# A linear-attention stage regrouped: 256 rows of each of two sequences, side by side in the partition halves

## The chip, the cores and the metric

The kernel runs on one NeuronCore of a Trainium2 chip. The core has five engines with instruction queues of their own: TensorE (PE in the profile; PEld is its loading of stationary operands), VectorE (DVE), ScalarE (ACT), GpSimd (POOL) and SyncE (SP, which here only issues DMAs). They meet through semaphores. The metric is the time of one execution in microseconds on the device; a run is repeated and the median compared. A profiled execution gives the trace; its span runs from the first to the last instruction.

## The reference

`x` is (4, 1024, 128) in float32. Four residual layers follow one another; the change is in the first two, and only in the first one's arithmetic order.

```python
# layer 1: linear attention, B=4, T=1024, D=128, H=64; xn = layernorm(x)
q, k, v = phi(xn @ W_q), phi(xn @ W_k), xn @ W_v        # phi(a) = elu(a) + 1
S_t = S_{t-1} + k_t v_t^T ;  z_t = z_{t-1} + k_t         # per sequence
o_t = (S_t q_t) / max(z_t . q_t, 1e-6)
x = x + o @ W_o
# layer 2: mixture of experts, E=8, top-1; xn = layernorm(x)
logits = xn @ router_W + router_b ; e = argmax(logits) ; gate = softmax(logits)[e]
x = x + gate * (relu(xn @ W1[e] + b1[e]) @ W2[e] + b2[e])
# layer 3: a gated token mix with a scan over time; layer 4: the experts again
```

## The kernel before

The 4096 rows are 32 tiles of 128. A **group** is four tiles, 512 rows in a row of one sequence, so a sequence has two groups and there are eight (`NG`). All work of a layer is written out by hand as slots, one list per engine: in slot `k` of `attn_slot` each engine does steps of several groups, `project_qk(k)`, `project_out(k-2)`, `score_and_turn(k-1)` and so on for PE, `add_attention(k-2)`, `mask_scores(k-1)`, `phi(k)`, `scan_z(k)` for DVE. Within an engine this order is fixed; between engines `wait_ge` on a counting semaphore holds a step until its input is there and the buffer it writes is free.

For a group the steps are these. ACT normalises the rows (`norm`), PE turns them (`transpose_x`), ACT copies them out (`evac_xT`). `project_qk` makes q in partitions 0 to 63 and k in 64 to 127 of `bank[1]`, 512 columns; `project_v` makes v in partitions 0 to 63 and the eight "old" router scores (those of the rows before attention's output is added) in 64 to 71 of `bank[2]`. ACT and DVE make phi of q and k (`phi_parts`, `phi`, tile `qk`). `score_and_turn` multiplies v by q for each tile (`L1621`), turns k (`turn_k`, `L1614`) and v with the old scores (`L1640`) so that rows lie in partitions (`kv`). DVE masks the scores (`am`, `L1088`). `updates_and_intra` forms the state updates (`L1660`, into partitions 0 to 63 of `bank[5]`) and the products inside a tile (`L1649`, into 64 to 127). `add_state` (`L1096`, `L1099`) adds the state that the sequence's first group left, and `read_inter` (`L1676`) multiplies it by q. `scan_z` (`L1114`) is the running sum of k on 64 partitions, `z_dot_q` on POOL (`L499`) multiplies it by q. `project_out` (`L1693`) takes both, stacked in `op`, through `wox`, which holds ones for the sum of z.q, `w_o`, and `w_o` times the router. `add_attention` (from `dmax`, `L950`) divides and adds to the rows.

Behind that, for the experts: `measure_choose_and_add_state` takes the row's moments, the logits and the one-hot choice `oh` (`L902`), `count` on PE (`L1586`, `L1590`) counts choices, `placed` gives each row its place, and POOL sends rows to a sorted buffer in HBM, tile by tile (`send_tiles`). Column `IDC` of the rows holds each row's number in `x`; the experts' results are scattered by it. The first expert tiles start when the first four groups have been sent.

SP issues all loads in one list: x, the output weights, the mixing weights (`rwo`, `rwr`, `rwv`, `vec`), then `b2b`, `w1all`, `w2s`. PE waits for the mixing weights in `setup_transposes`, which stands inside `score_and_turn(0)`. `warm_up` and `keep_clock` are matmuls that only keep TensorE busy.

Every float32 matmul appears in the trace as two passes, a transpose as one.

## Time and profile before

| | us |
|---|---|
| median of 3 runs (295.75 to 297.28) | 297.17 |
| the profiled execution | 295.25 |
| its span, first to last instruction | 293.5 |
| mean granted TensorE clock, share of 2.4 GHz | 0.994 |
| busy in the span: PE / DVE / POOL / ACT | 276.7 / 231.8 / 225.1 / 187.5 |

The attention stage is the first 77 us of the span. "Busy" counts an engine's own instructions; issuing DMAs, waiting and branching are not in it. A duration of a matmul in the trace includes its way through the array, so passes that follow one another overlap in the records.

### The profile page before, as it was taken

How to read it: one execution, taken by the hardware profiler on the slowest of the kernel's cores; microseconds unless marked ns; L12 is line 12 of the kernel's file. 1: busy time of each engine (PE TensorE's matmuls, PEld its weight loads, DVE VectorE, ACT ScalarE, POOL GpSimd, SP SyncE). 2: the span in 40 equal slices, each digit the busy share in tenths (PEclk: the TensorE clock that was granted, in tenths of full speed). 3: DMA queues.
4: the chain of work that ended last, by engine and by line, in shares of the span. 5: the costliest groups of instructions: out<-in, count | busy, mean ns of one | idle time of the engine just before them, and what ended most of it. 6: DMA issues, size and time to landing. Idle time of an engine off the chain costs nothing.

```text
span 293.5 us, 7743 instructions
## 1 busy us (share of the span) xinstructions
PE 276.7 (94%) x2177; PEld 243.1 (83%) x2177; DVE 231.8 (79%) x1019; ACT 187.5 (64%) x565; POOL 225.1 (77%) x302
## 2 busy tenths in 40 slices
PE   7999999988789999999999999999899999999994
PEld 7666666666489999999996479988698999999994
DVE  4889799999688698777874278999965997777773
ACT  2776666540289788888881166755378887666661
POOL 3967378889768888888555584788878888889775
PEclk9999999999799999999999999999999999999999
DMA  6998910000341563542100920011315235432210
GB/s 177 236 352 239 109 33 31 28 28 30 75 96 47 122 127 87 115 100 67 40 24 5 245 48 0 28 40 37 82 59 122 65 103 123 110 89 72 65 40 6
DMA packets 32522, 25.70 MB, mean 88 GB/s; under 512 B 6001, under 2 KB 28786, under 8 KB 32481
## 3 DMA queue, kind: packets, MB, share of 16 engines
q1 hardware_dynamic: 27328, 16.54, 25.5%
q0 software_dynamic: 4576, 8.57, 8.7%
...
q14 instruction: 23, 0.18, 0.2%
q10 hardware_dynamic: 576, 0.10, 0.2%
...
## 4 chain that ended last, share of the span: by engine, by line
PE 66%; DVE 17%; POOL 5%; issue 4%; DMA 3%; ACT 3%; SPq 0%; POOLq 0%; ACTq 0%
PE pair L1835 21%; PE pair L1821 13%; PE bank L1821 6%; PE bank L1706 4%; POOL sorted L517 3%; PE bank L1811 3%; PE pair L1748 3%; PE pair L1701 2%; PE pair L1601 2%; PE pair L1755 2%; DVE zT L1114 2%; DMA xs<-sorted 2%; PE pair L1693 2%; DMA sorted<-rows,place 2%; PE bank L1576 2%
## 5 line engine op out<-in xcount | busy, mean ns | idle before, releaser
L1835 PE MATMUL pair<-w2s,hT 128*128 x624 | 82.9, 276 | 0.3
L517 POOL DMA_INDIRECT sorted<-rows,place x64 | 66.7, 1043 | 18.3 <-issue 14.6
L1835 PEld LDWEIGHTS pair<-w2s,hT 128*128 128x128 f32 x624 | 75.7, 192 | 0.9 <-issue 0.6
L1821 PE MATMUL pair<-xsT,w1s 128*128 128x128 f32 x406 | 57.0, 276 | 0.9 <-ACT xsT L770 0.9
L1821 PEld LDWEIGHTS pair<-xsT,w1s 128*128 128x128 f32 x406 | 50.9, 192 | 2.0 <-issue 1.0
L693 ACT COPY w1s<-w1all 128x516 f32 x78 | 49.7, 638 | 0.6 <-issue 0.6
L540 POOL DMA_INDIRECT x_mid<-ys,xs x39 | 38.4, 985 | 14.4 <-DVE ys L1378 9.8
L540 POOL DMA_INDIRECT out<-ys,xs x39 | 38.4, 985 | 9.1 <-issue 7.2
L770 ACT COPY xsT<-bank 128x128 f32<-128x128 f32 x78 | 20.8, 266 | 36.8 <-PE bank L1811 35.7
L1368 DVE SCALAR_TENSOR_TENSOR ys<-pair,xs 128x128 f32<-128x128 f32 x78 | 26.9, 345 | 18.3 <-PE pair L1835 18.1
L775 ACT ACTIVATE hT<-pair,w1s 128x128 f32<-128x128 f32 x117 | 34.7, 374 | 1.1 <-PE pair L1821 1.1
L775 ACT ACTIVATE hT<-bank,w1s 128x128 f32<-128x128 f32 x109 | 32.6, 377 | 0.0
L1338 DVE TENSOR_SCALAR xsn<-xs 128x128 f32<-128x128 f32 x78 | 27.9, 360 | 5.6 <-DMA xs<-sorted 5.6
L1349 DVE SCALAR_TENSOR_TENSOR xs<-b2b,xs 128x128 f32<-128x128 f32 x78 | 27.3, 349 | 6.1 <-issue 3.3
L1821 PE MATMUL bank<-xsT,w1s 128*128 128x128 f32 x218 | 30.8, 276 | 0.4 <-ACT xsT L770 0.4
L491 POOL TENSOR_TENSOR rows<-veps,neg_half 128x4 f32<-128x4 f32 x16 | 21.3, 1334 | 9.0 <-ACT veps L649 8.8
L1358 DVE TENSOR_SCALAR hT<-pair,w1s 128x128 f32<-128x128 f32 x86 | 27.5, 345 | 0.6
L1821 PEld LDWEIGHTS bank<-xsT,w1s 128*128 128x128 f32 x218 | 27.4, 192 | 0.7 <-ACT xsT L770 0.7
L1811 PE MATMUL bank<-ident,xsn 128*128 128x128 f32 x78 | 21.4, 274 | 0.6 <-DVE xsn L1338 0.6
...
L637 ACT COPY xnT<-bank 128x512 f32<-128x512 f32 x16 | 9.5, 592 | 14.8 <-PE bank L1576 14.7
L1748 PE MATMUL pair<-wx,xnT 128*128 128x256 f32 x64 | 15.7, 389 | 0.7 <-ACT xnT L637 0.7
...
## 6 DMA issues: line engine op xcount, KB each, us to landing
...
sorted<-rows,place POOLq DMA_INDIRECT x64, 2.4
x_mid<-ys,xs POOLq DMA_INDIRECT x39, 2.6
```

The source lines that it names most:

```text
L517: pool.indirect_dma_start(sorted_rows[l], bass.IndirectOffsetOnAxis(ap=place[:, t:t + 1], axis=0), rows[:, t, :], None).then_inc(s_sent[l] ...
L540: pool.indirect_dma_start(x_new[l], bass.IndirectOffsetOnAxis(ap=xs[b][:, IDC:IDC + 1].bitcast(I32), axis=0), ys[b][:, 0:(XM, D)[l]], None ...
L693: nc.scalar.copy(w1s[i % NW][:], w1all[:, bass.ds(e, 1), :].rearrange("p o f -> p (o f)")).then_inc(s_w1, 1)
L775: last = nc.scalar.activation(hT[i % NB][:, c], bank[2 + i % 2][:, c * P:(c + 1) * P], ACT.Relu, bias=w1s[i % NW][:, DF + c:DF + c + 1])
L1338: nc.vector.tensor_scalar(xsn[i % NB][:], xs[b][:, 0:D], xs[b][:, MEAN:MEAN + 1], xs[b][:, RSTD:RSTD + 1], ALU.subtract, ALU.mult).then_in ...
L1349: nc.vector.scalar_tensor_tensor(out=xs[b][:, 0:D], in0=b2b[:, bass.ds(e, 1), :].rearrange("p o d -> p (o d)"), scalar=xs[b][:, GATE:GATE ...
L1358: last = nc.vector.tensor_scalar(hT[i % NB][:, c], bank[4 + i % 2][:, f:f + P], w1s[i % NW][:, DF + c:DF + c + 1], 0.0, ALU.add, ALU.max)
L1368: nc.vector.scalar_tensor_tensor(out=ys[b][:, 0:D], in0=bank[6 + i % 2][:, 0:P], scalar=xs[b][:, GATE:GATE + 1], in1=xs[b][:, 0:D], op0=AL ...
L1748: nc.tensor.matmul(mix_to(g, j), xnT[p][:, j * P:(j + 1) * P], wx[:].rearrange("p w d -> p (w d)"), start=(j % 2 == 0), stop=False, skip_g ...
L1811: nc.tensor.transpose(bank[0][:, 0:P], xsn[i % NB][:], ident[:]).then_inc(s_xsT, 1)
L1821: mm = nc.tensor.matmul(bank[2 + 2 * half + i % 2][:, c * P:(c + 1) * P], w1s[i % NW][:, f:f + P], xsT[i % NB][:], start=True, stop=True)
L1835: mm = nc.tensor.matmul(bank[6 + i % 2][:, 0:P], hT[i % NB][:, c], w2s[:, bass.ds(e, 1), c, :].rearrange("p o d -> p (o d)"), start=(c == ...
```

## The change

A group becomes 256 rows of each of two sequences (`HW = 256`; four chunks in a sequence, `CHUNKS`). Tiles 0 and 1 of a group belong to the first sequence, tiles 2 and 3 to the second. What stood in 64 partitions by 512 columns now stands in 128 by 256, the first sequence in partitions 0 to 63 and the second in 64 to 127. q and k lie side by side in columns. The products of the two sequences are separate matmuls on different halves of TensorE's rows or columns: `project_qk` four with 64 stationary columns, scores, updates, intra and inter products one per sequence. The running state and the sum z go through four groups instead of two. k is turned two tiles at a time, v likewise, and the old scores are made with the router as the stationary operand (`wr32`, padded to 32 columns), one matmul per tile into its own 32 partitions, and are turned with the third transpose. In `project_out` the output and the sum z.q are no longer stacked: each tile takes one matmul from `ob` and one with a single moving column from `zq`. The groups' loads of x are two DMAs each; `IDC` gets the new order of rows and, between the layers, the old one again.

```diff
-vT = [sb(f"vT{p}", [VC, GW]) for p in range(2)]
-kv = [sb(f"kv{p}", [P, GT, KC]) for p in range(2)]
-zT = [sb(f"zT{p}", [H, GW]) for p in range(2)]
-op = [sb(f"op{p}", [P, GW]) for p in range(2)]
+vT = [sb(f"vT{p}", [P, HW + P]) for p in range(2)]
+kt = [sb(f"kt{p}", [P, GT // 2, P]) for p in range(2)]
+vt = [sb(f"vt{p}", [P, 3, P]) for p in range(2)]
+zT = [sb(f"zT{p}", [P, HW]) for p in range(2)]
+zq = [sb(f"zq{p}", [P, HW]) for p in range(2)]
+ob = [sb(f"ob{p}", [P, HW]) for p in range(2)]
-state = [sb(f"state{p}", [H, GT, H]) for p in range(2)]
+state = [sb(f"state{p}", [P, GT // 2, H]) for p in range(2)]
...
 def _(sp):
     def load_x(l, g):
+        if l == 0:
+            pair, c = divmod(g, CHUNKS)
+            src = x_tok.rearrange("(r s c j p) d -> p r s c j d", s=2, c=CHUNKS, j=GT // 2, p=P)
+            for s in range(2):
+                t = g * GT + 2 * s
+                sp.dma_start(rows[:, t:t + 2, 0:D], src[:, pair, s, c]).then_inc(s_x_in[g], 16)
+            return
-        sp.dma_start(rows[:, tiles(g), 0:(D, XM)[l]], src[:, tiles(g), :]).then_inc(s_x_in[g], 16)
+        sp.dma_start(rows[:, tiles(g), 0:XM], src[:, tiles(g), :]).then_inc(s_x_in[g], 16)
     def load_xs(l, i):
...
-            sp.dma_start(wo_lo[:], w_o).then_inc(s_wo, 16)
+            sp.dma_start(wox[0:H, 0:D], w_o).then_inc(s_wo, 16)
...
-        nc.gpsimd.iota(column(IDC, slice(0, NT)).bitcast(I32), pattern=[[P, NT]], base=0,
+        nc.gpsimd.iota(column(IDC, slice(0, NT)).bitcast(I32),
+                       pattern=[[2 * T, B // 2], [HW, CHUNKS], [T, 2], [P, GT // 2]], base=0,
     def scales(S, b):
...
-        nc.gpsimd.tensor_tensor(op[p][0:H, :], zT[p][:], qk[p][0:H, :], ALU.mult).then_inc(AS["zq"], 1)
+        nc.gpsimd.tensor_tensor(zq[p][:], zT[p][:], qk[p][:, 0:HW], ALU.mult).then_inc(AS["zq"], 1)
     def old_logits(g):
-        nc.gpsimd.tensor_tensor(lold[:, tiles(g)], kv[g % 2][:, :, H:VC], per_tile(std1[:, tiles(g)], GT),
+        scores = vt[g % 2][:, 2].rearrange("p (j c) -> p j c", j=GT)[:, :, 0:E]
+        nc.gpsimd.tensor_tensor(lold[:, tiles(g)], scores, per_tile(std1[:, tiles(g)], GT),
     def rows_ready(l, S, g):
...
+    for s in range(len(STAGES[0])):
+        pool.wait_ge(s_sent[0][s], 16 * (rows_of_stage(0, s) + (s == 0)))
+    nc.gpsimd.iota(column(IDC, slice(0, NT)).bitcast(I32), pattern=[[P, NT]], base=0,
+                   channel_multiplier=1).then_inc(s_const, 1)
+    pool.wait_ge(s_const, 3)
...
-        nc.scalar.copy(vT[g % 2][:], bank[2][0:VC, :]).then_inc(AS["v"], 1)
+        nc.scalar.copy(vT[g % 2][:], bank[2][:, 0:HW + P]).then_inc(AS["v"], 1)
     def evac_kv(g):
-        nc.scalar.copy(kv[g % 2][:, :, VC:KC], bank[1][:, 0:GT * H].rearrange("p (j c) -> p j c", j=GT))
-        nc.scalar.copy(kv[g % 2][:, :, 0:VC], bank[3][:, 0:GT * VC].rearrange("p (j c) -> p j c", j=GT)
+        nc.scalar.copy(kt[g % 2][:], bank[1][:, 0:HW].rearrange("p (j c) -> p j c", c=P))
+        nc.scalar.copy(vt[g % 2][:], bank[3][:, 0:3 * P].rearrange("p (j c) -> p j c", c=P)
     def evac_o(g):
-        nc.scalar.copy(op[g % 2][H:P, :], bank[5][H:P, :]).then_inc(AS["oe"], 1)
+        nc.scalar.copy(ob[g % 2][:], bank[5][:, HW:GW]).then_inc(AS["oe"], 1)
     def turned_weights():
...
+    act.wait_ge(s_zeroed, 2)
+    act.wait_ge(s_wc_act, 1)
+    nc.scalar.copy(wr32[:, 0:E], wc[:, 3 * H:3 * H + E]).then_inc(s_wc_act, 1)
...
-        nc.vector.tensor_tensor(am[:], bank[4][:].rearrange("p (j t) -> p j t", j=GT),
-                                causal[:].unsqueeze(1).to_broadcast([P, GT, P]), ALU.mult).then_inc(AS["am"], 1)
+        for s in range(2):
+            last = nc.vector.tensor_tensor(am[:, 2 * s:2 * s + 2],
+                                           bank[4 + s][:, 0:HW].rearrange("p (j t) -> p j t", t=P),
+                                           causal[:].unsqueeze(1).to_broadcast([P, GT // 2, P]), ALU.mult)
+        last.then_inc(AS["am"], 1)
     def add_state(g):
-        n = GT if g % 2 == 0 else GT - 1
+        n = 2 if g % CHUNKS < CHUNKS - 1 else 1
-        upd = bank[5][0:H, 0:H * n].rearrange("v (j k) -> v j k", j=n)
-        if g % 2 == 0:
-            nc.vector.tensor_copy(state[0][:], upd).then_inc(AS["state"], 1)
+        upd = bank[4][:, HW:HW + H * n].rearrange("v (j k) -> v j k", j=n)
+        if g % CHUNKS == 0:
+            nc.vector.tensor_copy(state[g % 2][:, 0:n], upd).then_inc(AS["state"], 1)
-            nc.vector.tensor_tensor(state[1][:, 0:n], upd, state[0][:, GT - 1:GT].to_broadcast([H, n, H]),
+            nc.vector.tensor_tensor(state[g % 2][:, 0:n], upd, state[1 - g % 2][:, 1:2].to_broadcast([P, n, H]),
     def phi(g):
...
-        nc.vector.tensor_tensor_scan(zT[p][:], ones_col[H:P, 0:1].to_broadcast([H, GW]), qk[p][H:P, :],
-                                     0.0 if p == 0 else zT[0][:, GW - 1:GW], ALU.mult, ALU.add
+        nc.vector.tensor_tensor_scan(zT[p][:], ones_col[:, 0:1].to_broadcast([P, HW]), qk[p][:, HW:GW],
+                                     0.0 if g % CHUNKS == 0 else zT[1 - p][:, HW - 1:HW], ALU.mult, ALU.add
     def attn_slot(k):
...
     def turn_output_weights():
-        nc.tensor.transpose(bank[3][:, 0:H], wo_lo[:], ident[0:H, 0:H]).then_inc(s_wc_pe, 1)
+        nc.tensor.transpose(bank[3][:, 0:H], wox[0:H, 0:D], ident[0:H, 0:H]).then_inc(s_wc_pe, 1)
     def router_weights():
-        pe.wait_ge(s_wc_act, 2)
-        nc.tensor.matmul(bank[3][H:P, H:H + E], woT[:], wc[:, 3 * H:3 * H + E], start=True, stop=True
-                         ).then_inc(s_wc_pe, 1)
+        pe.wait_ge(s_wc_act, 3)
+        for s in range(2):
+            last = nc.tensor.matmul(bank[3][s * H:(s + 1) * H, H:H + E], woT[:], wc[:, 3 * H:3 * H + E],
+                                    start=True, stop=True)
+        last.then_inc(s_wc_pe, 1)
     def transpose_x(S, g):
...
-        nc.tensor.matmul(bank[1][:], wc[:, 0:2 * H], xnT[g % 2][:], start=True, stop=True
-                         ).then_inc(AS["qkp"], 1)
+        for w in range(2):
+            for s in range(2):
+                last = nc.tensor.matmul(bank[1][s * H:(s + 1) * H, w * HW:(w + 1) * HW], wc[:, w * H:(w + 1) * H],
+                                        xnT[g % 2][:, s * HW:(s + 1) * HW], start=True, stop=True)
+        last.then_inc(AS["qkp"], 1)
     def project_v(g):
-        nc.tensor.matmul(bank[2][0:VC, :], wc[:, 2 * H:3 * H + E], xnT[g % 2][:], start=True, stop=True
-                         ).then_inc(AS["vp"], 1)
+        if g == 0:
+            pe.wait_ge(s_wc_act, 2)
+        for s in range(2):
+            nc.tensor.matmul(bank[2][s * H:(s + 1) * H, 0:HW], wc[:, 2 * H:3 * H],
+                             xnT[g % 2][:, s * HW:(s + 1) * HW], start=True, stop=True)
+        for j in range(GT):
+            last = nc.tensor.matmul(bank[2][32 * j:32 * (j + 1), HW:HW + P], wr32[:],
+                                    xnT[g % 2][:, j * P:(j + 1) * P], start=True, stop=True)
+        last.then_inc(AS["vp"], 1)
     def score_and_turn(g):
         def turn_k(j):
-            t = slice(j * P, (j + 1) * P)
-            nc.tensor.transpose(bank[1][:, j * H:(j + 1) * H], qk[p][H:P, t], ident[H:P, H:P])
+            nc.tensor.transpose(bank[1][:, j * P:(j + 1) * P], qk[p][:, HW + j * P:HW + (j + 1) * P], ident[:])
-        for j in range(GT):
+        after(pe, AS["oe"], g)
+        after(pe, AS["state"], g)
+        for j in range(GT // 2):
-            last = nc.tensor.matmul(bank[4][:, t], vT[p][0:H, t], qk[p][0:H, t], start=True, stop=True)
-            if j == GT - 1:
-                last.then_inc(AS["scores"], 1)
-            if g == 0:
-                continue
-            if j == 1:
-                after(pe, AS["kv"], g)
-                pe.wait_ge(AS["rel"], min(g + 2, NG))
-            if j >= 1:
-                turn_k(j - 1)
+            for s in range(2):
+                h = slice(s * H, (s + 1) * H)
+                last = nc.tensor.matmul(bank[4 + s][:, t], vT[p][h, t], qk[p][h, t], start=True, stop=True)
+        last.then_inc(AS["scores"], 1)
-            pe.wait_ge(AS["rel"], 2)
-            for j in range(GT - 1):
-                turn_k(j)
-        turn_k(GT - 1)
-        for j in range(GT):
+        after(pe, AS["kv"], g)
+        pe.wait_ge(AS["rel"], min(g + 2, NG))
+        for j in range(GT // 2):
+            turn_k(j)
+        for j in range(3):
-            last = nc.tensor.transpose(bank[3][:, j * VC:(j + 1) * VC], vT[p][:, t], ident[0:VC, 0:VC])
+            last = nc.tensor.transpose(bank[3][:, t], vT[p][:, t], ident[:])
     def updates_and_intra(g):
-        n = GT if p == 0 else GT - 1
-        def intra(j):
-            t = slice(j * P, (j + 1) * P)
-            nc.tensor.matmul(bank[5][H:P, t], kv[p][:, j, VC:KC], am[:, j], start=(j == 0), stop=False,
-                             skip_group_check=True)
-        pe.wait_ge(AS["kv"], g + 1)
-        after(pe, AS["state"], g)
-        pe.wait_ge(AS["am"], g + 1)
-        after(pe, AS["oe"], g)
-        for j in range(GT):
-            if j == 1:
-                intra(1)
-            if j < n:
-                last = nc.tensor.matmul(bank[5][0:H, H * j:H * n].rearrange("v (i k) -> v i k", k=H),
-                                        kv[p][:, j, 0:H], kv[p][:, j:j + 1, VC:KC].to_broadcast([P, n - j, H]),
+        n = 2 if g % CHUNKS < CHUNKS - 1 else 1
+        def update(j):
+            for s in range(2):
+                h = slice(s * H, (s + 1) * H)
+                last = nc.tensor.matmul(bank[4][h, HW + H * j:HW + H * n].rearrange("v (i k) -> v i k", k=H),
+                                        vt[p][:, j, h], kt[p][:, j:j + 1, h].to_broadcast([P, n - j, H]),
-            if j != 1:
-                intra(j)
+        def intra(j):
+            for s in range(2):
+                h = slice(s * H, (s + 1) * H)
+                nc.tensor.matmul(bank[5][h, HW + j * P:HW + (j + 1) * P], kt[p][:, j, h], am[:, 2 * s + j],
+                                 start=(j == 0), stop=False, skip_group_check=True)
+        pe.wait_ge(AS["kv"], g + 1)
+        pe.wait_ge(AS["am"], g + 1)
+        for j in range(n):
+            update(j)
+        for j in range(GT // 2):
+            intra(j)
     def read_inter(g):
-        for j in range(GT):
-            if p == 0 and j == 0:
+        for j in range(GT // 2):
+            if g % CHUNKS == 0 and j == 0:
-            before_t = state[p][:, j - 1] if j > 0 else state[0][:, GT - 1]
-            last = nc.tensor.matmul(bank[5][H:P, t], before_t, qk[p][0:H, t], start=False,
-                                    stop=(j == GT - 1), skip_group_check=True)
+            for s in range(2):
+                h = slice(s * H, (s + 1) * H)
+                before_t = state[p][h, 0] if j == 1 else state[1 - p][h, 1]
+                last = nc.tensor.matmul(bank[5][h, HW + j * P:HW + (j + 1) * P], before_t, qk[p][h, t],
+                                        start=False, stop=(j == 1), skip_group_check=True)
     def project_out(g):
...
-            pe.wait_ge(s_wc_act, 3)
-        for j in range(GT):
-            last = nc.tensor.matmul(bank[6 + j // 2][:, YC * (j % 2):YC * (j % 2 + 1)],
-                                    op[p][:, j * P:(j + 1) * P], wox[:], start=True, stop=True)
+            pe.wait_ge(s_wc_act, 4)
+        for j in range(GT // 2):
+            t = slice(j * P, (j + 1) * P)
+            for s in range(2):
+                h = slice(s * H, (s + 1) * H)
+                nc.tensor.matmul(bank[6 + s][:, YC * j:YC * (j + 1)], ob[p][h, t], wox[h, :],
+                                 start=True, stop=False, skip_group_check=True)
+            for s in range(2):
+                h = slice(s * H, (s + 1) * H)
+                last = nc.tensor.matmul(bank[6 + s][:, YC * j + D:YC * j + D + 1], zq[p][h, t], ones_col[h, 0:1],
+                                        start=False, stop=True, skip_group_check=True)
     def warm_up(n):
```

## Rows read from the trace of the kernel before

**Rows 1.** Windows from `dmax` to `dmax`: busy us (instructions) of PE, PEld, DVE, ACT, POOL; clock, DMA.
```profile
23.65:30.50 6.85, 6.13 (x45) 4.13 (x45) 5.40 (x22) 4.54 (x12) 6.51 (x7) 1.00 0.87 217
30.50:60.10 29.60, 28.06 (x237) 20.26 (x238) 27.80 (x128) 18.85 (x49) 21.90 (x22) 1.00 0.28 47
60.10:67.54 7.44, 6.26 (x59) 4.70 (x60) 6.98 (x33) 2.36 (x7) 6.64 (x7) 1.00 0.09 29
67.54:77.59 10.05, 7.40 (x53) 5.56 (x51) 7.82 (x39) 2.31 (x6) 8.10 (x9) 0.87 0.10 29
```

**Rows 2.** Timeline of DVE, one slot: start us, duration us, instruction, [idle before, releaser].
```profile
45.26 0.15 DVE L950 TENSOR_SCALAR dmax<-pair 128x4 f32<-128x4 f32 x1
...
46.79 0.68 DVE L1088 TENSOR_TENSOR am<-pair,causal 128x512 f32<-128x512 f32 x1
...
49.26 0.42 DVE L1096 COPY state<-pair 64x256 f32<-64x256 f32 x1 [0.52 <-PE pair L1660]
...
50.09 0.19 DVE L902 TENSOR_TENSOR oh<-rev,top 128x32 bf16<-128x32 f32 x1
...
51.63 1.28 DVE L1114 TENSOR_TENSOR_SCAN zT<-ones_col,zT,qk 64x512 f32<-64x512 f32 x1
52.94 0.16 DVE L950 TENSOR_SCALAR dmax<-pair 128x4 f32<-128x4 f32 x1
```

**Rows 3.** Timeline of PE, the same slot.
```profile
45.57 0.27 PE L1621 MATMUL pair<-qk,vT 64*128 64x128 f32 x1
45.62 0.22 PE L1614 MATMUL pair<-ident,qk 64*128 64x64 f32 x1
45.68 0.27 PE L1621 MATMUL pair<-qk,vT 64*128 64x128 f32 x1
...
46.22 0.47 PE L1640 MATMUL bank<-ident,vT 72*128 72x72 f32 x4
...
47.92 0.43 PE L1660 MATMUL pair<-kv 128*64 128x256 f32 x1
47.92 0.43 PE L1649 MATMUL pair<-am,kv 128*64 128x128 f32 x2
48.18 0.38 PE L1660 MATMUL pair<-kv 128*64 128x256 f32 x1
...
49.73 0.87 PE L1676 MATMUL pair<-qk,state 64*64 64x128 f32 x6 [0.51 <-DVE state L1096]
50.53 0.19 PE L1586 MATMUL pair<-oh,before 128*128 128x32 bf16 x1
...
50.67 1.10 PE L1601 MATMUL pair<-xnT,wc 128*128 128x512 f32 x2
51.61 1.10 PE L1693 MATMUL pair<-wox,op 128*128 128x137 f32 x8
52.63 0.60 PE L1621 MATMUL pair<-qk,vT 64*128 64x128 f32 x3
```

**Rows 4.** Timeline of ACT, the same slot.
```profile
50.64 0.58 ACT L676 COPY op<-pair 64x512 f32<-64x512 f32 x1
```

**Rows 5.** Timeline of all engines, in the last slot.
```profile
69.62 1.28 POOL L499 TENSOR_TENSOR op<-zT,qk 64x512 f32<-64x512 f32 x1
69.69 1.24 DVE L1233 SCALAR_TENSOR_TENSOR ntile<-posb,whole 1x8 f32<-1x8 f32 x1
```

**Rows 6.** Timeline of all engines, start of the kernel (SPq: issues of SP).
```profile
3.74 3.68 SPq L367 DMA_DIRECT2D rows<-in_L_attn_a_x  x6
...
10.10 0.43 SPq L391 DMA_DIRECT2D vec<-in_L_attn_b_time_mix_r  x1
...
15.07 0.33 PE L1799 MATMUL pair<-ident,rwo 128*128 128x128 f32 x1
```

**Rows 7.** Instructions of line L391, the `vec` loads.
```profile
DMA to landing us min/median/max: 2.7/2.9/3.0
```

**Rows 8.** Timeline of POOL, between the layers.
```profile
164.28 0.23 POOL L469 TENSOR_SCALAR veps<-rows 128x4 f32<-128x4 f32 x1 [4.01 <-DMA rows<-x_mid]
```

More of the change, by code:

```diff
@@ L90, in hybrid_block @@
     YC = P + 1 + E
-    VC = H + E
-    KC = VC + H
+    HW = GW // 2
+    CHUNKS = T // HW
+    assert B % 2 == 0
     LASTB = len(ROUTE_BATCHES) - 1
@@ L153, in hybrid_block @@
         wc = sb("wc", [P, 3 * H + E])
-        wo_lo = sb("wo_lo", [H, D])
+        wr32 = sb("wr32", [P, 32])
         woT = sb("woT", [P, H])
@@ L467, in scales @@
                     for g in groups:
-                        pool.wait_ge(s_x_in[g], 32)
+                        pool.wait_ge(s_x_in[g], 48)
                     nc.gpsimd.tensor_scalar(veps1[:, t], column(P + 1, t), EPS, None, ALU.add).then_inc(BS["ve1"], 1)
@@ L683, in router_weights @@
                 act.wait_ge(s_wc_pe, 3)
-                nc.scalar.copy(wox[H:P, D + 1:YC], bank[3][H:P, H:H + E]).then_inc(s_wc_act, 1)
+                nc.scalar.copy(wox[:, D + 1:YC], bank[3][:, H:H + E]).then_inc(s_wc_act, 1)
             def copy_w1(l, i):
@@ L838, in first_moments @@
             def first_moments(g):
-                dve.wait_ge(s_x_in[g], 16)
+                dve.wait_ge(s_x_in[g], 32)
                 moments(AS, 1, g)
@@ L1520, in _ @@
             dve.wait_ge(s_zeroed, 1)
-            nc.vector.memset(wox[0:H, D:D + 1], 1.0).then_inc(s_zeroed, 1)
+            nc.vector.memset(wr32[:], 0.0).then_inc(s_zeroed, 1)
             nc.vector.memset(sc[0][:, 0:1], 0.0)
@@ L1896, in _ @@
             keep_clock(8)
-            pe.wait_ge(s_x_in[0], 32)
+            pe.wait_ge(s_x_in[0], 48)
             keep_clock(3)
```

## The prediction

> **What bounds the kernel now.** I read the busy shares by stage first, for the nine slots of the attention loop [rows 1]. The reader is to see three engines nearly full: over the four slots from 30.50 to 60.10 PE is busy 28.06 of 29.60 us, DVE 27.80, POOL 21.90, and the granted clock is 1.00 (2.4 GHz). A busy share does not say which engine sets the pace, so next I followed one slot in the timelines of DVE and PE [rows 2, 3]. A slot runs from one `dmax` (L950) to the next, 45.26 to 52.94, 7.68 us. In DVE's part the one-hot rows `oh` (L902) end at 50.28, 5.02 after the slot's start, of which 0.52 is a wait for PE's state updates; from there DVE needs 2.66 us more (phi, placing, and the 1.28 us `scan_z`) to reach the next `dmax`. On PE a second chain leaves from the same `oh`: the count (L1586) starts at 50.53, `project_qk` at 50.67, `project_out` at 51.61, and its last pass ends at 52.71, 2.43 us after `oh`. `dmax` needs both. DVE's leg is the longer by only 0.23 us. That is the point of this case: whatever DVE saves behind `oh` beyond that is a wait for `project_out`, unless PE's leg shrinks too.
>
> **The change, part by part.**
>
> *DVE.* `scan_z` goes from 64x512 to 128x256. With a fixed part of 0.15 (what the 128x4 `dmax` takes [rows 2]) it is 0.15 + 1.13/2 = 0.72; a pure half would be 0.64, so between 0.56 and 0.64 is saved; I take 0.56. The mask becomes two instructions of half the size: 0.68 [rows 2] pays its fixed part twice, +0.15 at most and 0 at least; I take +0.06, since neighbours overlap. The state (256 or 192 columns, now 128 or 64) saves 0.06 to 0.21; I take 0.13 in such a slot as this. `oh` then ends 5.02 - 0.52 + 0.06 - 0.13 = 4.43, say 4.4 us after the slot's start, once nothing waits for PE. DVE alone would make a slot of 4.4 + 2.66 - 0.56 = 6.5.
>
> *Does the 0.52 wait go?* PE's updates and intra products now stream 192 and 256 columns in each of two column halves where one half had 640 (the passes from 47.92) [rows 3]; at 0.21 us a 256-column pass (48.18 less 47.92 is 0.26 with the start-up) the updates take 0.32, not 1.07, and their semaphore no longer waits for the intra products. They start when the mask is done, about 2.4 after `dmax`, and end at 3.0; DVE asks for them at 3.4. The wait goes. If the logits passes ahead of them ran one after another (8 passes of 128 columns at 0.11, not 2) it would come back at about 0.2.
>
> *PE, whether pairs run side by side.* Everything above needs the two sequences' matmuls to overlap. For column halves the trace shows it: an update pass and an intra pass both start at 47.92. For row halves also: `turn_k` (rows 64 to 127) starts at 45.62 between two score passes 0.11 us apart (45.57, 45.68), and does not slow them [rows 3].
>
> One row goes further. The second pass of the first update starts at 48.18, 0.26 after the intra product that stands behind it in the program [rows 3]. [...]
>
> *PE's leg behind `oh`.* `project_qk` streams 4 x 256 columns in each column half, as many as the two 512-column passes in 0.94 us (50.67 to 51.61) [rows 3]; its change of shape adds about 0.06. A pass has a tail of 0.16 behind its columns (0.27 long, 0.11 apart). A change of shape is a gap of 0.09 (L1676 ends at 50.60, less the tail 50.44, and L1586 starts at 50.53), and the pass behind it can be 0.11 slower (three scores take 0.60, not 0.49) [rows 3]. `project_out` took 1.10 to its last end: eight passes of 137 columns at 0.117 and a tail. Now each row half has four such passes, 0.47, and four with one moving column. The trace has no one-column pass; the nearest are the 72-column transposes, four in 0.47 with the tail [rows 3], under 0.08 each; the other end is nothing at all, and above, 0.117 each as if the stationary load set it. I take 0.06, 0.24 in all. A new change of shape (column halves to row halves) is taken at 0.2. So 0.2 + 0.47 + 0.24 + 0.16 = 1.07. The leg is 2.43 + 0.06 - 0.03 = 2.46: it does not shrink. PE now also waits there for `evac_o`, but that copy (0.58 at 50.64 [rows 4]) only gets smaller and ends before `project_qk` does.
>
> A steady slot is therefore 4.4 + 2.46 + 0.06 (sending the last pass's semaphore to DVE, an estimate) = 6.9. DVE idles 0.4 of it.
>
> *POOL.* `zq` (L499, 1.28 us [rows 5]) halves to about 0.7. POOL had 26 % idle in the four slots [rows 1], and each is now shorter by less than POOL's own saving, so I expect it to set nothing. But one collision goes: in the last slot DVE's first table step (L1233, 1x8) takes 1.24 us, beginning and ending with `zq` [rows 5]. With a `zq` that is shorter and earlier (POOL no longer runs late) I count 1.1 of it as gained, 0 if they still meet.
>
> *SP.* The loads of `x` for layer 0 are two DMAs per group, so SP issues eight more. The six issues from 3.74 take 3.68, 0.61 each; the `vec` load at 10.10 takes 0.43 [rows 6]. So all behind them in the queue comes 3.4 to 4.9 later; I take 4.4. That `vec` load lands up to 3.0 later [rows 7], near 13.1; now 17.5. PE needs it at 15.07 (L1799, `setup_transposes` [rows 6]), and behind that instruction stand the turns of group 0, `transpose_x(2)`, `project_v(1)` and the updates; ACT's `evac_kv` and DVE's `mix_weights`, mask and state wait for those. That is 2.4 us later. The first slots give back about as much: two scans (1.1), updates that end 0.75 sooner, `inter` with two passes per half rather than six in all. I put the first `dmax` where it is, 23.65, with +-1. The load of group 0 itself may land 0.5 later; it is hidden behind the twelve warm-up matmuls. The remaining w2 loads have tens of us.
>
> *The rest.* A small copy more on ACT and one small matmul more for the router, both in the set-up: inside the +-1. The second iota on POOL stands ahead of `scales(BS, 0)`, which waits 4.01 us for `x_mid` [rows 8]; without that cover it would cost its own time, a fraction of a us.
>
> **The sum.** Slot 2 (6.85 [rows 1]) has no `oh`; its chain is state, `inter`, `project_qk`, `project_out`. `inter` took 0.87 for six passes with the tail, eight in the odd groups; it now has four per half, -0.43: 6.45, saving 0.40. Slots 3 to 6: 29.60 to 4 x 6.92 = 27.7, saving 1.9. Slot 7 has no `project_qk` behind `oh`, so DVE sets it: 7.44 to 6.5, saving 0.94. Slot 8: 10.05 to 9.0, saving 1.05. The start: 0. Together 4.3. What follows (project_out(7), the experts) starts by these ends and is shifted whole: the sends to the first expert stages hang on the same `oh` and place steps. The profiled execution took 295.25 around its span of 293.5, so 291.0; the median of three was 297.17, 1.9 above it, and I forecast by the median: 297.17 - 4.3 = **292.9 us**.
>
> **Rivals.**
> - *DVE sets the slots* (one-column passes nearly free, changes of shape at 0.09, `project_out` 0.4 shorter): slots at 6.5, 1.7 more saved in slots 3 to 6 and 0.2 in slot 2, 291.0. For it: the short transposes; against: the first pass after a change of shape is slow in the rows.
> - *Pairs staggered by a pass*: `project_qk` +0.21, `project_out` +0.12 in slots 2 to 6, a little in 7 and 8: 2.0 less, 294.9. Against it: 48.18 behind 47.92.
> - *The ends go badly*: `vec` at 18.0 on the path, and `zq` still meets the table step: 4.3 - 1 - 1.1 = 2.2 saved, 295.0.
> - *The other side: row halves don't overlap when both are matmuls.* The row shown pairs a matmul with a transpose, and no row pairs two products. Then `project_out` is 0.71 longer, `inter` 0.44, scores 0.44: slots 3 to 6 at 7.74 (`inter` delays the count by 0.1; +1.4), slot 2 +0.75, slot 7 -0.7, slot 8 +0.8 (at the lower clock its passes cost double): 2.2 slower, 299.4. It decides once PE's leg is about 0.7 longer in each of the six slots, which eats the 4.3.
> - *The clock falls.* PE drops about 1.3 us of passes a slot (scores 0.4, `inter` 0.4, updates and intra 0.3, `project_v` 0.2) and the slot only 0.5, so it idles about 1 us of it. In the last slot the clock mean is 0.87 [rows 1], after PE stood idle for DVE. If it fell to 1.2 GHz in three slots, PE's 2 us behind `oh` double in each: 6 us, 298.7.
>
> **How the numbers follow.** Chances: forecast 0.45; DVE sets the slots 0.17; staggered 0.12; ends 0.08; row halves serial 0.10; clock 0.08. A measurement of this kernel tells about 0.5 %, 1.5 us, from no change. The first four are faster by more than that, save some of their lower tails: 0.78. Same 0.07, slower 0.15. The range 289.0 to 297.0 takes in the first four with the +-1 of the start and leaves 0.18 to the last two. The likeliest alone: 291.4 to 294.4.
>
> **What would show it.** Right: `dmax` to `dmax` near 6.9 in slots 3 to 6, `dmax` waiting some 0.4 for the last pass of `project_out`, `scan_z` near 0.7, no wait of the state for PE, PE waiting for `vec` in `setup_transposes`, passes of the two halves starting together. Wrong: `project_out` passes of the halves one behind the other; a clock of 0.5 inside the loop; `dmax` of group 0 later than 25.

## The result, and the profile after

The median went from 296.46 us (4 runs) to **288.27 us** (286.45 to 289.95, 4 runs), ratio 0.974, interval 0.970 to 0.979. Beside later experiments the changed kernel ran again: 287.42 (6 runs) against 295.62 (11 runs), 0.974 (0.970 to 0.978). The forecast was 292.9, range 289.0 to 297.0: right in direction, but 0.7 below the range, with a gain of 8 us where 4.3 were forecast. Medians and ratios, here and below, are of runs within 1.5 % of the fastest of their kernel. The profiled execution took 286.45 us around a span of 284.7, 8.8 less than before. Windows from `dmax` to `dmax`, columns as in [rows 1], slots 2, 3 to 6, 7 and 8:

```profile
21.61:28.01 6.40, 6.01 (x77) 4.16 (x75) 4.87 (x22) 4.38 (x12) 4.90 (x8) 1.00 1.13 325
28.01:55.27 27.26, 25.51 (x322) 17.99 (x322) 24.94 (x132) 17.17 (x49) 17.80 (x21) 1.00 0.48 90
55.27:61.69 6.42, 5.17 (x73) 3.74 (x73) 6.24 (x34) 2.01 (x7) 4.93 (x7) 1.00 0.11 34
61.69:69.29 7.60, 5.69 (x59) 3.84 (x58) 6.57 (x41) 2.07 (x6) 5.67 (x7) 1.00 0.14 43
```

Set against the terms of the sum:

| term | forecast | saved |
|---|---|---|
| start, to the first `dmax` (23.65 to 21.61) | 0 | 2.04 |
| slot 2 (6.85 to 6.40) | 0.40 | 0.45 |
| slots 3 to 6 (29.60 to 27.26) | 1.9 | 2.34 |
| slot 7 (7.44 to 6.42) | 0.94 | 1.02 |
| slot 8 (10.05 to 7.60) | 1.05 | 2.45 |
| behind it (215.91 to 215.41) | 0 | 0.50 |
| sum | 4.3 | 8.8 |

The steady slots came out nearly as worked out. The error lies at the two ends. The 0.50 behind the last `dmax` is no more than profiles of one kernel differ by there (215.83, 215.91 and 217.13 in three of the kernel before with and without small edits). One steady slot in the timeline of DVE:

```profile
41.63 0.16 DVE L970 TENSOR_SCALAR dmax<-pair 128x4 f32<-128x4 f32 x1 [0.53 <-PE pair L1734]
...
43.18 0.75 DVE L1109 TENSOR_TENSOR am<-pair,causal 128x256 f32<-128x256 f32 x2
...
45.11 0.28 DVE L1119 COPY state<-pair 128x128 f32<-128x128 f32 x1
...
45.81 0.19 DVE L922 TENSOR_TENSOR oh<-rev,top 128x32 bf16<-128x32 f32 x1
...
47.26 0.74 DVE L1137 TENSOR_TENSOR_SCAN zT<-ones_col,zT,qk 128x256 f32<-128x256 f32 x1
48.44 0.16 DVE L970 TENSOR_SCALAR dmax<-pair 128x4 f32<-128x4 f32 x1 [0.43 <-PE pair L1734]
```

The state waits for nothing now ([rows 2]: 0.52), the scan takes 0.74, and `dmax` waits 0.43 for the last pass of `project_out`. PE's leg behind that `oh`, in the timeline of PE:

```profile
46.10 0.18 PE L1611 MATMUL pair<-oh,before 128*128 128x32 bf16 x1 [0.22 <-issue]
...
46.30 1.08 PE L1628 MATMUL pair<-xnT,wc 128*64 128x256 f32 x8
47.31 0.50 PE L1730 MATMUL pair<-wox,ob 64*128 64x137 f32 x4
47.65 0.28 PE L1734 MATMUL pair<-ones_col,zq 64*128 64x1 f32 x4
47.79 0.48 PE L1730 MATMUL pair<-wox,ob 64*128 64x137 f32 x4
48.11 0.28 PE L1734 MATMUL pair<-ones_col,zq 64*128 64x1 f32 x4
```

A pass is one record of PE. Over both whole traces every float32 matmul of the program has two and every transpose one. In the trace before, the 32 matmuls of `project_out` are x64 (L1693), the 28 of `read_inter` x56 (L1676), the 312 of the experts' second product x624 (L1835), but the 32 transposes of `turn_k` x32 (L1614) and the 64 of `transpose_x` x64 (L1576); in the trace after, the 32 matmuls of `project_qk` are x64 (L1628) and the 16 transposes of `turn_k` x16 (L1648). Records of passes overlap: those of `project_out` in [rows 3] are 0.28 long and 0.117 apart.

The last slot, of POOL, DVE and PE; and the last `project_out` of the kernel before, with a window from the fall of its clock at 75.05 to the rise at 78.46:

```profile
62.49 0.74 POOL L510 TENSOR_TENSOR zq<-zT,qk 128x256 f32<-128x256 f32 x1
...
63.90 0.14 DVE L1256 SCALAR_TENSOR_TENSOR ntile<-posb,whole 1x8 f32<-1x8 f32 x1
...
67.79 0.19 PE L1611 MATMUL pair<-oh,before 128*128 128x32 bf16 x1 [1.88 <-DVE oh L922]
...
68.10 0.51 PE L1730 MATMUL pair<-wox,ob 64*128 64x137 f32 x4
```

```profile
75.09 0.21 PE L1586 MATMUL pair<-oh,before 128*128 128x32 bf16 x1 [1.79 <-DVE oh L902]
...
75.32 2.16 PE L1693 MATMUL pair<-wox,op 128*128 128x137 f32 x8
```

```profile
75.05:78.46 3.41, 3.37 (x15) 2.85 (x16) 1.58 (x11) 1.01 (x3) 2.41 (x3) 0.50 0.17 41
```

The reader is to see two things. `ntile` no longer meets `zq` (0.14, not 1.24 [rows 5]). And before, the granted clock was 0.50 right where `dmax` waited for PE: `project_out` took 2.16, against 1.10 in a steady slot [rows 3], its passes 0.228 apart and not 0.117. The traces give the clock as a share alone: 1.00, and 0.50 where the recorded texts say 1.2 GHz. In this profile of the changed kernel the clock stayed at 1.00 there. At the start, POOL and DVE of the kernel before, then SP's queue and PE of the changed one:

```profile
19.26 1.28 POOL L499 TENSOR_TENSOR op<-zT,qk 64x512 f32<-64x512 f32 x1
...
19.80 1.30 DVE L1107 SCALAR_TENSOR_TENSOR qk<-ex,rl 128x512 f32<-128x512 f32 x1
```

```profile
4.72 6.07 SPq L374 DMA_DIRECT2D rows<-in_L_attn_a_x  x12
...
13.25 0.43 SPq L401 DMA_DIRECT2D vec<-in_L_attn_b_time_mix_r  x1
...
15.37 0.33 PE L1840 MATMUL pair<-ident,rwo 128*128 128x128 f32 x1 [1.35 <-DMA vec<-in_L_attn_b_time_mix_r]
```

Before, phi of group 1 (L1107) began while `zq` of group 0 ran, and took 1.30. The halved loads cost 0.51 each to issue, the six whole ones 0.61 [rows 6], and `vec` landed 2.1 after its issue, not 2.9 [rows 7].

### The profile page after: what moved, and what is told of

The parts are those of the page before. It is cut to its first block, busy times and chain, and to the rows that moved or that the text cites. A ratio compares the mean times of both kernels' runs of the same rounds, so it can differ in the third digit from the quotient of the medians.

```text
span 284.7 us, 8106 instructions
## 1 busy us (share of the span) xinstructions
PE 267.9 (94%) x2347; PEld 236.7 (83%) x2347; DVE 225.8 (79%) x1027; ACT 184.4 (65%) x566; POOL 216.3 (76%) x303
## 4 chain that ended last, share of the span: by engine, by line
PE 60%; DVE 15%; POOL 9%; issue 6%; SPq 4%; DMA 4%; ACT 1%; POOLq 0%
PE pair L1876 21%; PE pair L1862 13%; PE bank L1862 7%; POOL sorted L529 6%; PE bank L1747 3%; SPq L374 3%; PE bank L1852 3%; PE pair L1789 3%; DVE rows L987 2%; PE pair L1796 2%; DMA xs<-sorted 2%; PE pair L1628 2%; POOL rows L502 2%; DVE stats L1002 2%; DMA sorted<-rows,place 2%
## 5 line engine op out<-in xcount | busy, mean ns | idle before, releaser
L1361 DVE TENSOR_SCALAR xsn<-xs 128x128 f32<-128x128 f32 x78 | 28.6, 369 | 5.9 <-DMA xs<-sorted 5.8
L502 POOL TENSOR_TENSOR rows<-veps,neg_half 128x4 f32<-128x4 f32 x16 | 17.0, 1064 | 12.3 <-ACT veps L666 12.1
```

The lines of the kernel that those rows point to most:

```text
L1361: nc.vector.tensor_scalar(xsn[i % NB][:], xs[b][:, 0:D], xs[b][:, MEAN:MEAN + 1], xs[b][:, RSTD:RSTD + 1], ALU.subtract, ALU.mult).then_in ...
```

## The experiments

All times are medians beside runs of the kernel before (295.5 to 295.9); slots are read from one profile each, and `..` in an edit stands for what is left out of a line. Five profiles whose start is the same code (the changed kernel twice, and three versions below) have the first `dmax` at 21.61, 21.86, 21.84, 21.98 and 22.31, so a start is known to some 0.4 only. Their first twelve warm-up matmuls, 24 passes, take 4.57, 4.57, 5.29, 5.41 and 5.49: from the second on the passes stand 0.213 apart until the granted clock rises to 1.00, and 0.112 from then on. Between profiles with a warm-up of like length the change saves 1.8 at the start, not 2.04 (5.18 before and 5.29 after: 23.65 and 21.84; 5.49 and 5.49: 24.07 and 22.31).

**Who sets the steady slots.** A second scan on DVE:

```
+ nc.vector.tensor_tensor_scan(scratch[:], ones_col.., qk[p][:, HW:GW], 0.0, ALU.mult, ALU.add)
  nc.vector.tensor_tensor_scan(zT[p][:], ...
```

> The changed kernel with a second scan of the same size (128x256, into a scratch tile that nothing reads) in front of each `scan_z`: DVE gets about 0.70 us more per slot, PE and the rest get nothing. Theory (PE's leg behind `oh`, that is count, `project_qk` and `project_out`, sets slots 3 to 6, and `dmax` waits 0.43 to 0.53 us for it): the slack takes most of it, slots 3 to 6 go from 6.82 to about 7.05, slot 2 and the start grow by up to 0.7 each, the whole by 1.5 to 2.5 us. Rival (DVE sets the slots): 0.70 more in each of the slots 2 to 7 and in the start, 4.5 to 5 us, `dmax` waiting for nothing in either kernel.

```profile
28.89:56.18 27.29, 25.54 (x324) 18.04 (x324) 26.88 (x136) 17.20 (x49) 17.51 (x21) 1.00 0.43 82
```
```profile
41.28 0.68 DVE L1138 TENSOR_TENSOR_SCAN scratch<-ones_col,qk 128x256 f32<-128x256 f32 x1
41.88 0.67 DVE L1140 TENSOR_TENSOR_SCAN zT<-ones_col,qk 128x256 f32<-128x256 f32 x1
42.49 0.16 DVE L971 TENSOR_SCALAR dmax<-pair 128x4 f32<-128x4 f32 x1
```

Slots 3 to 6 take 27.29 with the second scan and 27.26 without, 6.82 each where 7.05 was expected. The scan's 0.60 a slot (41.28 to 41.88) went into the wait at `dmax`, which is gone: DVE had that slack, and PE's leg had set these slots. Slot 7, which has no `project_qk` behind `oh`, grew by 0.41 (289.54 us).

The opposite test shortens PE's leg. `project_qk` of the next group goes ahead of `read_inter`, first with the count ahead of `inter` too, then with the count left behind it:

```
  updates_and_intra(k - 1)
+ if 3 <= k < NG - 1: project_qk(k + 1)      # and not at the head of slot k + 1
  read_inter(k - 1)                          # first version: behind the count
  if 3 <= k < NG: pe.wait_ge(AS["xnew"], k - 1); count(...)
```

> The changed kernel with `project_qk` of the next group and the count moved ahead of `read_inter` on PE, for groups 4 to 7: `project_qk` then fills the 0.43 us in which PE waits for the state, and behind `oh` there are only the count, `inter` and `project_out`. Theory (PE's leg sets slots 3 to 6, with 0.43 to 0.53 of slack on DVE): slots 3 to 6 go from 6.82 to 6.4 to 6.6, `dmax` waits 0.2 or less, 1 to 1.5 us gained in all. Rival (PE is bound by its whole work in the slot, not by the leg): slots 3 to 6 within 0.1 of 6.82.

```profile
46.55 0.18 PE L1611 MATMUL pair<-oh,before 128*128 128x32 bf16 x1
...
46.75 0.44 PE L1710 MATMUL pair<-qk,state 64*64 64x128 f32 x4
47.66 0.51 PE L1730 MATMUL pair<-wox,ob 64*128 64x137 f32 x4 [0.47 <-ACT ob L693]
```

Slots 3 to 6 took 27.50, no gain. (The 291.01 us hold more than that: the clock fell at 61.62, to 0.50, and slots 7 and 8 took 7.74 and 9.97.) I had left out that `inter` behind the count puts `evac_o` behind `oh` as well: a chain of the same length took the place of the one removed.

> The changed kernel with `project_qk` of the next group moved ahead of `read_inter`, and the count left behind `read_inter`. In the run with the count ahead of `inter` the wait only moved: `evac_o` on ACT and then `project_out` stood behind `oh` instead of `project_qk`, a leg of 2.52 us as before. Here the leg behind `oh` holds only the count and `project_out`, about 1.6 us with `evac_o` in time. Theory (PE's leg sets the slots): slots 3 to 6 go from 6.82 to 6.4 to 6.55, set by DVE, `dmax` waits 0.1 or less, 1.2 to 1.6 us gained in these slots. Rival (something else, POOL or ACT, holds them at 6.8): within 0.1 of 6.82. PE then idles longer in the slots; if the clock falls for it, slot 7 or 8 gives back 1 to 2 us.

```profile
28.72:55.09 26.37, 24.68 (x323) 18.07 (x323) 25.16 (x132) 16.97 (x49) 17.12 (x20) 1.00 0.47 83
```

Slots of 6.59, the wait of `dmax` down to 0.07 to 0.21. Now DVE does set them, as the first rival had it (6.5). The slots gain 0.9, where 1.2 to 1.6 were expected; the clock fell at 69.42 in that profile, and the median, 287.68, does not show the gain.

**Halves in turn.** `project_qk`, the scores and `project_out` issue all matmuls of one sequence and then all of the other:

```
- for j in range(GT // 2): for s in range(2): matmul(bank[6 + s].., ob[p][h, t], wox[h, :])
+ for s in range(2): for j in range(GT // 2): matmul(bank[6 + s].., ob[p][h, t], wox[h, :])
```

> The changed kernel with the order of the issue changed in `project_qk`, the scores and `project_out`: all matmuls of the first sequence, then all of the second, instead of the two in turn. Same matmuls, same banks. If a matmul starts only when those ahead of it in the program have started (program order across the halves), two by two become three in a row: `project_qk` 0.4 longer, `project_out` and the scores 0.2 to 0.3 each, slots 3 to 6 at 7.4 to 7.7, 4 to 5 us in all. If each half of the array has a queue of its own, nothing changes: slots 6.8, within 0.5 us.

```profile
48.63 1.09 PE L1628 MATMUL pair<-xnT,wc 128*64 128x256 f32 x8
49.66 0.50 PE L1730 MATMUL pair<-wox,ob 64*128 64x137 f32 x2
49.99 0.28 PE L1732 MATMUL pair<-ones_col,zq 64*128 64x1 f32 x2
50.13 0.50 PE L1730 MATMUL pair<-wox,ob 64*128 64x137 f32 x4
```

Neither theory. `project_qk` takes 1.09, and 1.08 with the halves in turn: its third matmul, on the other column half, started at 48.651, 0.013 behind the first (48.638), past the second, which started at 49.120. In `project_out` the other sequence's first matmul stands fifth; it started at 50.142, with the third (50.136) and past the fourth (50.453), but not with the first (49.659), so one block ran alone, and slots 3 to 6 grew to 7.30, by 0.49 each (292.64 us). Measured here, a matmul passed one waiting ahead of it, on column halves (48.651) and on row halves (50.142), but not three.

**POOL against DVE.** In the kernel before, `zq` in four pieces; in the changed kernel, a second product ahead of `zq`:

```
+ for i in range(4): nc.gpsimd.tensor_tensor(op[p][0:H, t], zT[p][:, t], qk[p][0:H, t], ALU.mult)   # before
+ nc.gpsimd.tensor_tensor(scratch[p][:], zT[p][:], qk[p][:, 0:HW], ALU.mult)                         # changed
```

> The kernel before, with `zq` cut into four instructions of 128 columns on POOL, one behind the other. Theory (a POOL product and a DVE instruction with both operands in SBUF shut each other out while they run, so DVE waits for the rest of one POOL instruction): `ntile` goes from 1.24 to 0.3 to 0.5, phi of group 1 from 1.30 to 0.7 to 1.0; 0.8 to 1.3 us gained at these two places, less what four fixed parts cost POOL (its `zq` 1.28 to about 1.6). Rival (`ntile` was long for something else): it stays near 1.24.

```profile
70.61 1.69 POOL L501 TENSOR_TENSOR op<-zT,qk 64x128 f32<-64x128 f32 x4
70.69 0.45 DVE L1236 SCALAR_TENSOR_TENSOR ntile<-posb,whole 1x8 f32<-1x8 f32 x1
71.17 0.38 DVE L1241 TENSOR_SCALAR ntile<-ntile 1x8 f32<-1x8 f32 x1
71.59 0.34 DVE L1246 TENSOR_TENSOR_SCAN cumt<-ones_col,ntile 1x8 f32<-1x8 f32 x1
71.97 0.43 DVE L1254 TENSOR_TENSOR past<-slot_i,cumt 1x72 f32<-1x72 f32 x1
```

`ntile` shrank to 0.45 as expected, but the next three steps each met the next piece: the four lose 0.92 where one had lost 1.10 (they take 0.14, 0.16, 0.16 and 0.22 in the changed kernel). Slot 8 stayed at 9.94, the median at 296.02. At the start phi of group 1 took 0.89, not 1.30, but the first `dmax` came at 24.12, no earlier. Cutting `zq` in four gained nothing. POOL was held up as well: in the changed kernel `zq` of group 0 took 1.16 beside phi and the second scan (0.68 and 1.10), and 0.73 where it was issued ahead of them (18.80 in its first profile, 17.03 in the version below). DVE steps with an operand in PSUM did not lengthen beside `zq`: `am` of the kernel before met it in five of eight slots and took 0.68 in all eight.

> The changed kernel with a second product of the size of `zq` (128x256, into scratch tiles that nothing reads) on POOL ahead of each `zq`: POOL's part at this place is as long as in the kernel before, about 1.4 us. Theory (the shorter `zq` is worth something only where it met a DVE instruction with two operands in SBUF: `ntile` in the last slot, phi of group 1 at the start): the steady slots stay at 6.8, the start grows by 0.3 to 0.7 and the first table step takes 0.3 to 1.2 instead of 0.14; POOL's sends after the loop come up to 1.4 later, so 1 to 2.5 us in all. Rival (POOL's load sets the slots or the sends throughout): the slots grow by 0.7 each, 5 us or more. Other rival (POOL has room everywhere and the collision was something else): under 0.5 us and `ntile` stays at 0.14.

```profile
64.89 0.74 POOL L511 TENSOR_TENSOR scratch<-zT,qk 128x256 f32<-128x256 f32 x1
65.08 0.58 DVE L1258 SCALAR_TENSOR_TENSOR ntile<-posb,whole 1x8 f32<-1x8 f32 x1
65.58 0.73 POOL L512 TENSOR_TENSOR zq<-zT,qk 128x256 f32<-128x256 f32 x1
65.69 0.65 DVE L1263 TENSOR_SCALAR ntile<-ntile 1x8 f32<-1x8 f32 x1
```

The two steps take 1.23 instead of 0.30: 0.93 is back, the steady slots stay at 6.81, and the median is 292.46. This slot took 9.37, since the clock fell as well (69.73, ahead of `project_out`). The whole grew by 4 to 5 us, where 1 to 2.5 were expected: against the changed kernel's first profile 1.20 stands ahead of the first `dmax` (0.50 beside 22.31, which has the same warm-up of 5.49), 1.77 in slot 8 and 2.85 behind the loop, where the clock stayed down until 76.55 and fell again at 209.67. What of the 2.85 is POOL's is not shown.

At the start, `zq` of group 0 went ahead of POOL's first indirect store (1.24 on POOL; in the kernel before it landed 6.1 after its issue, the 64 sends of `send_tiles` 2.4 in the median):

> The changed kernel with POOL's first indirect store (1.24 us, it only opens the path) moved behind `zq` of group 0 instead of in front of it. Theory (at the start `zq` of group 0 meets phi or the scan of group 1 on DVE, 0.3 to 0.4 us lost, 0.6 in the kernel before): `zq` runs from about 17.5, phi takes 0.68 and the scan 0.75, the first `dmax` 0.3 to 0.4 earlier than in the run of the unchanged kernel beside it. Rival (the collision is hidden: `dmax` waits for PE instead): the two instructions get shorter and the first `dmax` stays within 0.1.

```profile
18.87 1.10 DVE L1130 SCALAR_TENSOR_TENSOR qk<-ex,rl 128x512 f32<-128x512 f32 x1
```
```profile
19.06 0.68 DVE L1131 SCALAR_TENSOR_TENSOR qk<-ex,rl 128x512 f32<-128x512 f32 x1
```

Phi took 0.68 (second line), against 1.10 in the changed kernel without this edit (first line); from the state to `dmax` 2.85, not 3.20 (3.12 in the changed kernel's first profile). The collision was on the path and cost about 0.3. The median, 288.23, doesn't show it.

**The clock.** `keep_clock(2)` where PE stood idle ahead of the last count, in either kernel:

```
  if 0 <= k - 1: read_inter(k - 1)
+ if k == NG: keep_clock(2)
```

> The kernel before, with two more of its own filling matmuls (`keep_clock(2)`, four passes of 512 columns, 1.72 us) on PE in the last slot, after the last `inter` product, where PE stands idle for 1.75 us until the last `oh`. Theory (1.1 us of the 2.45 that the change gained in the last slot is the clock: before, it was at 1.2 GHz through the whole of the last `project_out` but one, whose passes came 0.228 us apart and not 0.117): these passes come 0.117 apart, the last slot goes from 10.05 to 8.8 to 9.0, and 1 to 1.6 us are gained in all. Rival (the change gained it by the shorter products alone): the last slot stays within 0.3 of 10.05.

```profile
73.71 1.98 PE L1706 MATMUL bank<-w2s,ident 128*128 128x512 f32 x4
...
75.79 1.17 PE L1693 MATMUL pair<-wox,op 128*128 128x137 f32 x8
```

Slot 8 went from 10.05 to 9.05 at a clock of 1.00; 294.98 us, ratio 0.9955 (0.9925 to 0.9985). One us of slot 8 had been the clock.

> The changed kernel with two more filling matmuls (1.72 us) on PE in the last slot, after the last `inter` product, where PE stands idle for 1.88 us. Theory (the idle stretch ahead of the last count is what lets the clock fall around the last `project_out` and the first expert matmuls, at 69.7 to 75.1 in all profiles so far but the changed kernel's first): no stretch at 0.5 between 60 and 80, the last slot 7.6, a median 0.5 to 1.5 us below the changed kernel's. Rival (the falls there have another cause): a stretch at 0.5 near 70 to 74 all the same.

No fall between 60 and 80, slot 8 7.51; 287.11 us, where the changed kernel had 287.42 and 288.27. Too little to tell by the time, and the changed kernel's own two profiles show no fall there either. All eighteen profiles together tell more: of the five with the filling matmuls none has a fall between 60 and 80, of the thirteen without them ten have.

**The start.** Five small loads ahead of the mixing weights, or the mixing weights ahead of the last `x` loads:

```
+ for i in range(5): sp.dma_start(spare[:, i:i + 1], mix_r..)      # vec_late
  for dst, src in ((rwo, rw_o), ..                                 # mix_first: moved to g == 6 of the x loop
```

> The changed kernel with five more small loads (128x1, into a tile that nothing reads) on SP's queue ahead of the mixing weights: they should put the issue of the last `vec` load about 2.2 us later, so that it lands near 17.5, where the prediction had put it. Theory (in the start only the arrival was mis-sized, its price was right): PE waits for it in `setup_transposes` until 17.5 instead of 15.37, the first `dmax` comes 1.9 to 2.2 us later, near 23.7, and so does the end. Rival (the start has slack behind that wait, the gain there came from elsewhere and would have come anyway): the first `dmax` moves by less than 0.7.

```profile
17.96 0.33 PE L1844 MATMUL pair<-ident,rwo 128*128 128x128 f32 x1 [4.01 <-DMA vec<-in_L_attn_b_time_mix_r]
```
```profile
19.00:22.50 3.50, 3.50 (x30) 2.13 (x30) 2.10 (x7) 1.99 (x6) 0.28 (x1) 0.51 0.90 312
```

PE started 2.59 later than in the changed kernel, the first `dmax` came at 25.40, where 23.7 was expected (292.75 us): the delay and about 1 us more. Behind those 4.01 us of idle the clock stood at 0.51 from 19.00 to 22.50.

> The changed kernel with the six loads of the mixing weights (`rwo` to `vec`) moved on SP's queue ahead of the `x` loads of groups 6 and 7. Theory (the start of the changed kernel hangs on SP's queue: PE waits 1.35 us for `vec`): the last `vec` load is issued 2.05 earlier, near 11.2, and lands near 13.4; PE waits for nothing there, the first `dmax` comes 1.0 to 1.4 earlier, near 20.4, and the end with it. Rivals: `x` of groups 6 and 7 lands too late for their moments (DVE waits for it; the gain is under 0.5), or POOL's sends, which gate the expert tiles of the second stage, take the gain back later.

```profile
16.08 0.26 DVE L1342 COPY rwoT<-pair 128x128 f32<-128x128 f32 x1
```

PE waited for nothing there (its transposes at 14.06), but DVE reached `rwoT` at 16.08, after the moments of groups 5 and 6; in the changed kernel at 16.07. First `dmax` 21.48: nothing gained (287.08 us, inside the spread of the changed kernel).

> The version with the mixing weights ahead of `x` of groups 6 and 7, and with the moments of groups 6 and 7 (2.35 us of DVE) one slot later each, those of 7 where DVE waits 1.39 us in slot 2; the POOL step that reads them one slot later too. With the loads alone moved, PE waited for nothing and the first `dmax` came only 0.13 earlier, because DVE was still at the moments of groups 5 and 6 until 16.07. Theory (the start of the changed kernel is bound by DVE's queue, and `vec` was hidden behind it but for 0.1): first `dmax` 0.9 to 1.3 earlier, near 20.4, slot 2 unchanged at 6.4, 1 us or so in all. Rival (another chain, ACT's `evac_kv` or the updates, is as long): under 0.5.

0.975 (0.968 to 0.982), no gain. The first `dmax` came at 22.40, behind a warm-up of 5.49, and so beside the 22.31 of the version above with that warm-up; slot 3 grew by 0.49. With the moments out of the way DVE waits 1.18 for PE, which has waited 0.40 for `xn` of group 2: another chain of the start, nearly as long.

**Together.** The changed kernel again, and three versions that combine edits:

> The changed kernel itself once more, unchanged, beside the others of this call. What is asked is how much of its 2.05 us at the start and of its 7.60 in the last slot belongs to the kernel and how much to that one execution: profiles whose start is the same code had the first `dmax` between 21.6 and 22.3. Expected: first `dmax` 21.5 to 22.4, slots 3 to 6 within 0.05 of 6.82, and a stretch at 1.2 GHz near 70 in this profile or in some of the timed runs; a median of 287 to 289.

> The changed kernel with the four edits together: mixing weights ahead of the last `x` loads, the moments of groups 6 and 7 later, `project_qk` ahead of `inter`, and the filling matmuls ahead of the last count. If each does what its theory says: start 1.0, slots 3 to 6 1.4, the clock 0.5 to 1, so 283.5 to 285.5 and a ratio to the kernel before of 0.955 to 0.962. If POOL's sends become the bound (they are back to back from 68 to 84 in the changed kernel) the gain shrinks to 1 us or less.

> The changed kernel with the mixing weights ahead of the last `x` loads, `project_qk` ahead of `inter`, and the filling matmuls ahead of the last count; the moments stay where they are (moved, they cost 0.45 in slot 3 and gained little at the start). Expected from the runs of each: start 0.1 to 0.3, slots 3 to 6 0.9, the clock 0.5 to 1: 285.5 to 286.5, with slots 3 to 6 at 6.58. If the version with the moments moved was better for it, this one is slower than 286.4 by 0.3 or more.

> The same three edits and the first indirect store behind `zq` of group 0. If the collision at the start is on the path, 0.3 to 0.4 us below the version with three edits: 285.2 to 286.1; if it is hidden, the same.

First `dmax` 21.86, slots 3 to 6 27.28, slot 8 7.59, median 287.42 for the changed kernel. The versions: 286.37 (ratio 0.969, 0.965 to 0.974), 286.90 (0.970) and 287.48 (0.971). From the first `dmax` to the last they take 47.08, 46.72 and 46.74, the changed kernel 47.68: those 0.6 to 1.0 us are there in each profile, but the intervals overlap, and no version is shown to beat it. None came down to the time expected of it.

## Why the prediction was wrong, and what in it was right

The mechanism of the steady slots was right; two terms of the sum were mis-sized, the start (forecast 0, saved 1.8 to 2.0) and slot 8 (forecast 1.05, saved 2.45).

- *DVE saves, PE's leg does not shrink.* Right: `oh` ends 4.37 behind `dmax` (forecast 4.4) and the last pass of `project_out` 2.39 later (2.46); `project_out` takes 1.08 (1.07), its one-column passes 0.28 of that, 0.14 for each block (0.24), the scan 0.74 (0.72), and `dmax` waits 0.43 to 0.53 (0.4). The change of shape between them, taken at 0.2 with no row to show it, cost 0.20: the first pass of `project_out` starts 0.31 behind the last of `project_qk`, whose passes stand 0.215 apart, and the second 0.22 behind that, not 0.117. The 0.06 to DVE, of which no row is the source either, was 0.05 (48.39 to 48.44). The second scan and the shorter leg show it from both sides.
- *Pairs run side by side.* Right, and both rivals against it fall: the first passes of the two halves start 0.007 apart in `project_qk` (46.302, 46.309) and 0.006 in `project_out` (47.317, 47.323). The stagger of a whole pass, 2.0 us by the rival's sum, was an estimate, and no run shows it in this order of issue. But it rests on the order of issue, as the halves in turn show, and my row (48.18 behind 47.92 [rows 3]) was a second pass of a matmul already begun.
- *"The start: 0".* **Failed.** It saved 2.04 in these profiles, 1.8 at a like warm-up. The debit was wrong: PE was to get `vec` at 17.5, 2.4 later than before, and got it at 15.37, 0.3 later. I put its issue 4.4 later, and it came 3.15 later, since a half load took 0.51 and not 0.61; and I kept a landing time of 3.0, where 2.1 was measured (the DMA column of a window over it shows 0.29, and 1.06 before). The late `vec` shows that the price of such a wait was no exaggeration. `vec` at 15.37 cost about nothing, since DVE was not ready either. The credit, 1.8 to 2.3 (2.4), was about right, though of another make-up: before, the state waited 0.96 for PE and now 0.30; before, phi of group 1 met `zq` and took 1.30, now 0.68, while now the second scan met it, 1.10.
- *"Slot 8: 10.05 to 9.0".* **Failed.** It saved 2.45, not 1.05. The collision went as forecast (1.1). But the mean clock of 0.87 stood in [rows 1], and I used it only for a rival against the change. Its price there, eight passes 0.228 apart and not 0.117, was 1.0 in the run that kept the clock up. The other 0.35 lies in smaller steps of DVE ahead of `oh`, which starts 5.85 behind `dmax`, not 7.31. That the clock stayed up is the change's in part only, and so in part luck: of the last 11 runs of the kernel before, ten have a mean clock below 0.996, of 10 of the changed kernel five. And a mean does not say where the clock fell: 0.994 goes with a fall at 75.05 alone (the kernel before) and with one at 203.72 alone (the version with the mixing weights first).
- *The size without the clock.* Six runs of the kernel before with a mean clock of 0.999 or more took 293.76 to 294.32 (median 294.07), five of the changed kernel 286.45 to 287.96 (286.75). That is 7.3 us, still 3 above the forecast, so the clock is the smaller part of the miss.
- *The base.* The forecast started from 297.17, the median of three runs; the sets of more runs gave 295.5 to 296.5. That put the forecast about 1 us too high, whatever the change saves.
- *The clock falls, as a rival.* In no profile did it fall in slots 2 to 6. In eight versions it fell between 61.6 and 73.6, in slots 7 and 8 or just behind them. (By its own terms this rival's time is 298.9, not 298.7.)
- *POOL sets nothing.* Right in the slots.

What stays open: why the clock of the changed kernel falls in one execution and not in the next, and why the warm-up is of such different length. The split of the `x` loads itself was not undone in a run.
